# First attention, three entries: where the layernorm's root and its normalised tiles are computed

## The reference

```python
def _layernorm(x, axis=-1, eps=1e-05):
    m = jnp.mean(x, axis=axis, keepdims=True)
    v = jnp.var(x, axis=axis, keepdims=True)
    return (x - m) / jnp.sqrt(v + eps)
...
x = _layernorm(x + _L0_attn_ref(x, ...), axis=-1)
x = _layernorm(x + _L0_ffn_ref(x, ...), axis=-1)
x = _layernorm(x + _L1_attn_ref(x, ...), axis=-1)
x = _layernorm(x + _L1_ffn_ref(x, ...), axis=-1)
```

## Time and profile before

| | us |
|---|---|
| three runs | 1034.5, 1035.62, 1036.26 |
| median | 1035.62 |
| profiled execution, span from first to last instruction | 1033.4 |
| the median less that span | 2.2 |
| first attention in the profiled execution, about | 29 to 299 |

### The profile page before, as it was taken

One profiled execution on the slowest core, in us unless ns is written; L12 is line 12 of the kernel. 1 busy time (PEld: TensorE's weight loads), 2 busy tenths in 40 slices (PEclk: granted clock), 3 DMA queues, 4 the chain that ended last, 5 costly groups with the idle time before them and its releaser, 6 DMA issues.

```text
span 1033.4 us, 18254 instructions
## 1 busy us (share of the span) xinstructions
PE 991.0 (96%) x6658; PEld 826.1 (80%) x6658; DVE 735.9 (71%) x2003; ACT 606.6 (59%) x1177; POOL 371.4 (36%) x646
## 2 busy tenths in 40 slices
PE   8999999989999898889999999999999999999997
PEld 6555655556658897778989999999999999999997
DVE  6676787767638779866557777766776876677764
ACT  5576657664359774455556666455666655466660
POOL 4455474562131574353722223322222232222600
PEclk9899999998999999999999999999999999999999
DMA  7100010012110001022201010010101011010101
GB/s 249 28 2 22 4 35 8 23 60 85 45 65 4 1 8 36 28 76 62 82 1 42 1 41 4 39 42 1 42 1 42 1 42 42 1 42 1 42 24 59
DMA packets 29234, 36.91 MB, mean 36 GB/s; under 512 B 1780, under 2 KB 26584, under 8 KB 29144
## 3 DMA queue, kind: packets, MB, share of 16 engines
q1 hardware_dynamic: 24728, 31.15, 9.5%
q10 hardware_dynamic: 4416, 4.59, 1.4%
HBM read 31.40 MB, written 4.20 MB: 34 GB/s over the span
## 4 chain that ended last, share of the span: by engine, by line
PE 56%; DVE 4%; POOL 2%; issue 1%; ACT 1%; DVEq 0%; POOLq 0%; ACTq 0%
PE ps L1947 25%; PE ps L1964 24%; PE ps L1837 2%; PE ps L1919 2%; DVE ln_stats L2366 1%; PE ps L1977 1%; PE ps L1888 1%; POOL hs L1734 1%; POOL x_b L1734 0%; PE ps L1851 0%; DVE amp L2402 0%; PE ps L1866 0%; PE ps L1879 0%; PE ps L1788 0%; DVE att L2458 0%
## 5 line engine op out<-in xcount | busy, mean ns | idle before, releaser
L2202 ACT ACTIVATE G<-ps,bias_col 128x512 f32<-128x512 f32 x192 | 135.9, 708 | 176.6 <-PE ps L1947 167.9
L1964 PE MATMUL ps<-w_h,G_h 128*128 128x256 f32 x736 | 204.3, 278 | 0.0
L1964 PE MATMUL ps<-w_l,G_h 128*128 128x256 f32 x736 | 204.0, 277 | 0.0
L1964 PE MATMUL ps<-w_h,G_l 128*128 128x256 f32 x736 | 204.0, 277 | 0.0
L2506 DVE TENSOR_TENSOR G_l<-G,G_h 128x512 fp32r<-128x512 f32 x192 | 155.8, 820 | 59.6 <-ACT G_h L2203 59.6
L1764 POOL TENSOR_TENSOR x_a<-xn,mlp_g 128x1024 f32<-128x1024 f32 x20 | 68.0, 3399 | 333.8 <-DVE xn L2534 333.8
L708 ACT ACTIVATE probs<-ps 128x512 f32<-128x512 f32 (+3 forms) x256 | 98.3, 441 | 96.5 <-PE ps L847 95.7
L1947 PE MATMUL ps<-xT_h,w_h 128*128 128x512 f32 x384 | 151.7, 395 | 0.2 <-issue 0.2
L1947 PE MATMUL ps<-xT_h,w_l 128*128 128x512 f32 x384 | 149.9, 390 | 0.0
L1947 PE MATMUL ps<-xT_l,w_h 128*128 128x512 f32 x384 | 149.5, 389 | 0.0
L1124 DVE CUSTOM_DVE_ANT_0 ps<-ps,q_mask 128x128 f32<-128x128 f32 (+3 forms) x256 | 120.8, 512 | 29.5 <-PE ps L836 29.0
(11 more groups left out here) (330 smaller groups left out, 2099.8 us busy)
## 6 DMA issues: line engine op xcount, KB each, us to landing
w_raw<-L_ffn_W_T SPq DMA_DIRECT2D x12, 1024.0 KB, 5.1
hs<-L_attn_hidden_states SPq DMA_DIRECT2D x8, 512.0 KB, 3.9
x_kept<-hs SPq DMA_DIRECT2D x4, 512.0 KB, 4.1
w_raw<-x_kept SPq DMA_DIRECT2D x2, 1024.0 KB, 5.3
out<-xn SPq DMA_DIRECT2D x3, 512.0 KB, 2.8
w_raw<-L_ffn_ent_w_T SPq DMA_DIRECT2D x1, 1024.0 KB, 9.8
w_raw<-L_ffn_ent_pw SPq DMA_DIRECT2D x1, 1024.0 KB, 12.0
heads_T<-neg_rows SPq DMA_DIRECT2D x64, 2.0 KB
```

The lines of the kernel that those rows point to most:

```text
L1964: mm = pe.matmul(ps[:, 4 + t // 2, (t % 2) * D:(t % 2 + 1) * D], x[b % 2][f][:, t * P:(t + 1) * P], w2_chunk(w, f), start=(k == 0), stop=( ...
L2202: act.activation(G32[n % 4], bank, ACT.Gelu, bias=bias)
```

## The change

In entries 1 to 3 of the first attention the layernorm of the batch before is spread over three engines:

- VectorE: one `bn_stats` in each of slots (3,1), (3,2), (4,0), (4,1) and the four `bn_aggr` in (4,2). Its nine root steps and its four `xn` tiles are gone there.
- ScalarE: in slot (4,3) the root, as Ln of variance plus eps and then Exp of -1/2 times that, 4 columns each. At the start the table set that holds both is preloaded, where an Exp instruction stood before.
- GpSimd: the four `xn` tiles, one in each of slots (5,0) to (5,3), after the slot's other steps. Keep tiles move to (6,1), (6,2), (6,3), (7,0), bias tiles from (5,1), (5,2), (5,3), (6,0) to (6,0), (7,1), (7,2), (7,3).

The layernorm of batch 3 after the entries stays on VectorE.

```diff
-BIAS_TILE_AT = ((5, 1), (5, 2), (5, 3), (6, 0))
-KEEP_TILE_AT = ((6, 2), (6, 3), (7, 0), (7, 1))
+STATS_AT = ((3, 1), (3, 2), (4, 0), (4, 1))
+MEAN_AT = (4, 2)
+ROOT_AT = (4, 3)
+NORM_TILE_AT = ((5, 0), (5, 1), (5, 2), (5, 3))
+KEEP_TILE_AT = ((6, 1), (6, 2), (6, 3), (7, 0))
+BIAS_TILE_AT = ((6, 0), (7, 1), (7, 2), (7, 3))
...
+        pool.memset(g.turns[:, 2:3], EPS).then_inc(s["g_eps"], 1)
...
+        def normalised_tile(b, t):
+
+            if t == 0:
+                pool.wait_ge(s["a_root"], b + 1)
+                pool.wait_ge(s["g_x1"], b + 1)
+            ins = pool.tensor_scalar(xn[:, 0, t, :], g.rsum[:, t, :], g.lnw["mv"][:, t, 0:1],
+                                     g.lnw["y"][:, t:t + 1], ALU.subtract, ALU.mult)
+            if t == RT - 1:
+                ins.then_inc(s["v_norm"], 1)
...
+                    if when != "first" and (p, r) in NORM_TILE_AT:
+                        normalised_tile(i - 1, NORM_TILE_AT.index((p, r)))
                     if when != "first" and (p, r) in KEEP_TILE_AT:
...
+        def root(b):
+
+            if b == 0:
+                act.wait_ge(s["g_eps"], 1)
+            act.wait_ge(s["v_mean"], b + 1)
+            act.activation(g.lnw["var"][:, :], g.lnw["mv"][:, :, 1], ACT.Ln, bias=g.turns[:, 2:3]
+                           ).then_inc(s["a_log"], 1)
+            act.wait_ge(s["a_log"], b + 1)
+            act.activation(g.lnw["y"][:, :], g.lnw["var"][:, :], ACT.Exp, scale=-0.5).then_inc(s["a_root"], 1)
...
-        act.activation(wave_phase[:, 2, 0:1], wave_phase[:, 3, 0:1], ACT.Exp)
+        act.preload_act_table_set("natural_log_exp_and_others")
...
+        def row_statistics(i, when, t):
+
+            if t % 2 == 0:
+                v.wait_ge(s["work_read"], WORK.number(i, when, ("out", t // 2)) + 1)
+            ins = v.bn_stats(g.lnw["stats"][:, t, :], g.rsum[:, t, :])
+            if t == RT - 1:
+                chain.step(ins)
+
+        def row_means():
+            chain.settle()
+            for k in range(RT):
+                ins = v.bn_aggr(g.lnw["mv"][:, k, :], g.lnw["stats"][:, k, :])
+            ins.then_inc(s["v_mean"], 1)
...
-                if (p, r) == (4, 0) and when != "first":
-                    norm = normalise(i, when)
-                next(norm, None)
-                next(norm, None)
-            assert next(norm, None) is None
+                if when != "first" and (p, r) in STATS_AT:
+                    row_statistics(i, when, STATS_AT.index((p, r)))
+                if when != "first" and (p, r) == MEAN_AT:
+                    row_means()
```

More of the change, by code:

```diff
@@ L271, in build @@
         g.last_b = put(nc, "last_b", g.small, 20 * D - 80 - D, [D])
-        g.turns = sb(top, nc, "turns", [P, 2])
+        g.turns = sb(top, nc, "turns", [P, 3])
         attention0(nc, A, g, top)
@@ L397, in attention0 @@
              "p_work work_read p_ex ex_read a_xT a_attT a_nT v_xT g_rope g_chain g_val a_stack stack_low "
-             "p_max v_max v_neg m_row0 m_row1 p_score a_exp g_sel p_out a_out v_chain v_norm g_x1 "
+             "g_eps v_mean a_log a_root p_max v_max v_neg m_row0 m_row1 p_score a_exp g_sel p_out a_out v_chain v_norm g_x1 "
              "phase_in v_turn a_sin v_mod mod_out mod_in small_in wave_rows_in path_in gate_in ent_in l1_in last_in "
@@ L765, in entry @@
                         matrix_high(MATRIX_HIGH_AT[p, r])
+                    if when != "first" and (p, r) == ROOT_AT:
+                        root(i - 1)
         def first_copies(t):
@@ L1258, in prepare, with normalise @@
                 yield
[L1260 to L1265, removed]
+        def row_statistics(i, when, t):
[9 more added lines that the diff above has]
+            ins.then_inc(s["v_mean"], 1)
+        def normalise():
+            v.wait_ge(s["v_tail"], 2 * KC)
             yield from layernorm_steps(v, chain, g.lnw, g.rsum, xn[:, 0, :, :], s["v_norm"],
-                                       (s["g_x1"], i))
+                                       (s["g_x1"], B))
         PREPARE_AT = ((1, 2), (1, 3), (2, 0), (2, 1), (2, 2), (2, 3), (3, 2), (3, 3), (4, 0), (5, 1), (5, 3), (6, 1),
@@ L1274, in entry @@
             slots = [(p, r) for p in range(PAIRS) for r in range(RT)]
-            norm = iter(())
             work_ahead = prepare()
@@ L1395, in _ @@
                             x_res[:, 2 * half:2 * half + 2, :], ALU.add).then_inc(s["v_tail"], 1)
-        for _ in normalise(B, "after"):
+        for _ in normalise():
             pass
```

## The result

The changed kernel takes 1039.68 us (median), the kernel before 1035.06 on the same chip: ratio 1.004, 95% interval 1.0027 to 1.0054, so slower by 4.6 us, or 0.4%. The profiled execution of the changed kernel has a span of 1037.9 us, that of before 1033.4: +4.5.

A forecast was written before the change was run, and what follows sets the result against it. TensorE, busy 96% of the span, was taken as the bound, its gaps setting the stage's length. Terms 1.6 + 1.7 + 0.4 - 0.5 + 1.1 = +4.3 us on the median 1035.62 gave 1039.9, range 1036.8 to 1042.7.

The forecast's parts named there:

- The stall: Slot (5,3), entries 1 and 2: three GpSimd tiles delay `k_stack`; TensorE idles some 3.3 us, losing 1.6 and 1.7 us.
- The tile's duration: GpSimd's `xn` tiles in pair 5: 1.22 us each, from eight such tiles in the trace, against 0.52 on VectorE.
- Statistics in pair 3: Slots (3,1) and (3,2), entries 1 and 2: one `bn_stats` in each frees score banks later, 0.2 us lost per entry.
- The clock: Behind slot (5,3): half clock after the idle time in both entries 1 and 2, one stretch more, +1.1 us (-1.1 to +2.2).
- Entry 3: Pair 5 gains about 1 us, the last select in pair 7 loses some 0.45: -0.5, between -1.0 and +0.3.
- The root on ScalarE: Slot (4,3): Ln 0.31 and Exp 0.20, 0.6 us together ahead of exponential (5,0), taken to cost nothing.
- GpSimd's backlog in pairs 6 and 7: Three more bias tiles make selects up to 0.7 us later, but value passes read them two slots later: taken at nothing.
- No further half-clock stretch: Rival, behind slot (5,3): the stall comes without one more slow stretch, 1038.8 us, or 1037.7; chance 0.19.
- Faster: Rival, `k_stack` of slot (5,3): GpSimd's tile is short there, 0.52 us by the line-rate rule, giving 1033.1 us; chance 0.07.
- point of decision: Slot (5,3): at a GpSimd tile of about 0.65 us `k_stack` lets TensorE go on as early as before.

The follow-up runs named there:

- filled run: Changed kernel plus, in entries 1 and 2, thirteen matmuls nobody reads ahead of TensorE's wait for the stack in slot (5,3): 1037.17 us, ratio 1.0012.
- Experiment 4: Changed kernel with all four `bn_stats` of each entry in slots (4,0) and (4,1), two in each, none in pair 3: 1040.64 us, ratio 1.0055.
- one tile ahead: Changed kernel with one GpSimd `xn` tile in slot (5,0), ahead of the stack, and three behind it in (5,3): 1032.87 us, ratio 0.9971.
- tiles on VectorE one per slot: Changed kernel with the four `xn` tiles done by VectorE instead of GpSimd, still one in each of slots (5,0) to (5,3): 1030.70 us, ratio 0.995.
- tiles in one slot: Changed kernel with the four `xn` tiles done by VectorE, all in slot (5,1): 1032.18 us, ratio 0.9965.
- the run with 0.79: Changed kernel with GpSimd doing columns 0 to 127 of each `xn` tile and VectorE the rest in the same slot: 1036.46 us, ratio 1.0013.
- the run with the tiles behind: Changed kernel with all four GpSimd `xn` tiles in slot (5,3), behind that slot's stack and select: 1029.78 us, ratio 0.9941.
- the run with the bias tiles back: Changed kernel with VectorE doing all four `xn` tiles in slot (5,1), and GpSimd's bias and keep tiles where the kernel before has them: 1034.94 us, ratio 0.9997.
- rearranged: Changed kernel with `xn` tiles behind the stack in (5,3), two `bn_stats` moved to (3,3), entry 3's bias tiles in pairs 5 and 6: 1028.77 us, ratio 0.9937.

## Why the prediction was right, point by point

- **The stall** was right in place and cause and nearly in size. Idle time 3.39 and 3.40 us where I said 3.3 (the terms that I gave for it, 1.7 and 1.5, make 3.2). The chain from GpSimd's first tile to the end of `k_stack` took 5.43 us against 5.63: a tile is 1.18 us from start to next start, not 1.22, and GpSimd came to it 0.15 us earlier, not 0.1. The loss at full clock is pair 5 of the filled run, 10.20 and 10.19 us, against 8.81: 1.39 us in each entry where the sum has 1.6 and 1.7.
- **The tile's duration**, taken from eight tiles of a later stage, held: 1.212 to 1.220 us for all twelve. The Trainium skill's GPSIMD Engine Reference, section 4.1, has one-input work on GpSimd at roughly line-rate; for this tile with its two pointers the trace disagrees (0.40 us on VectorE, and 1.217 on GpSimd), and the whole sign of the result hung on it. The 0.52 that I read for VectorE is a mean over four tiles, one of them drawn out by a neighbour (last section).
- **Statistics in pair 3**: +0.17 and +0.27 us, said 0.2. Experiment 4 shows that this is the price of those two `bn_stats`, and that moving them into pair 4 doesn't save it: it comes back in slot (5,0).
- **The clock** is the term that was mis-sized. I wrote +1.1, one stretch more at a price of 1.09, with +2.2 as the upper bound. The filled run gives 1.43 and 2.60 us for the changed kernel. Before, entry 2's pairs 5 and 6 take 18.07 us against entry 1's 16.68, so 1.39 was paid there already: the change adds 2.6 us, more than my bound. Two steps failed: the price, read from slot (6,0) to its end alone, left out the end of pair 5, which was slow too (9.09 against 8.81); and entry 2, where I counted no change, has a slow stretch twice as long as it had (206.40 to 213.10 in the window above, against 201.60 to 205.00).
- **Entry 3**: pair 5 gained 1.37 us (said 1), and the last select costs 0.35 us at the end (said 0.45): from slot (7,0) to the next stage's first matmul it is 5.89 us where it was 5.54, and TensorE now waits for it:

```profile
303.27 0.64 PE L889 MATMUL ps<-probs,val 128*32 128x256 f32 x8 [0.21 <-POOL probs L597]
```

- **The root on ScalarE** costs nothing. Ln and Exp stand ahead of exponential (5,0), no table load between them, and slot (5,0) is 1.74 us where it was 1.77:

```profile
131.69 0.34 ACT L764 ACTIVATE ln_var<-ln_mv,turns 128x4 f32<-128x4 f32 x1
132.07 0.20 ACT L767 ACTIVATE ln_y<-ln_var 128x4 f32<-128x4 f32 x1
132.18 1.07 ACT L725 ACTIVATE probs<-ps 128x512 f32<-128x512 f32 x2
```

- **GpSimd's backlog in pairs 6 and 7**: nothing, as taken; pair 7 is 7.38 us (7.37 before).
- **What the sum did not have.** Of the total, entry 1 (2.94) is the forecast's 2.9, though by other parts (1.39 of stall, 1.43 of clock, 0.17 of statistics); entry 2 is 1.0 us above its 1.9, the stretch up to entry 1 is 0.9 above its zero, and entry 3 is 1.7 below its -0.5. The last two are mostly half-clock stretches that none of my steps touches: one in pair 3 of entry 0 came (7.95 us, 6.41 before; the entry's first score matmul came 0.87 us earlier, which takes back part of it), the one in pairs 0 and 1 of entry 3 went (8.20 and 7.37 us, 9.44 and 7.63 before). Entry 0's pair 3, whose work is the same in all kernels of the table, is 6.4 to 6.5 us in nine of the twelve and 7.9 in three (changed, one tile ahead, tiles on VectorE one per slot); entry 3's pair 0 is 9.4 in three (before, one tile ahead, tiles in one slot) and 8.2 in nine. I can't say what sets them off. So the total of 4.3 against 4.5 is in part luck. By the terms it is: stall 2.8 (said 3.3), statistics 0.4 (0.4), entry 3 -1.0 (-0.5), clock 2.6 (1.1), and some -0.4 that no term had. The mechanism and the sign owe nothing to these errors that cancel.
- **The rivals.** "No further half-clock stretch" is what the filled run built: 1037.17, where I had 1038.8. "Faster" has no row for it: GpSimd's tile is 1.22 us. Its point of decision, 0.65, came from a loss of 1.7; with the 1.39 measured it would be 1.22 less 0.46, 0.76, for pair 5 alone, and the run with 0.79 fits that (8.92 us for pair 5, against 8.81). What a short tile itself would give stays unmeasured; the run with the tiles behind shows what the change is worth with no tile ahead of the stack, 5.7 us, which is more than the 2.5 of that rival.

## What to carry to other kernels

When work moves to an engine that is less busy on the average, look for the step in that engine's own queue which the bounding engine waits for, and count the idle time ahead of that step: here 0.77 us, and what went beyond it was paid in full. The same work one step further back in the queue, behind that step, turned 0.4% slower into 0.6% faster. And price a stall on TensorE with the slow stretch behind it, which here cost nearly as much again (2.6 us) as the stall made the two pairs longer (2.8).

## What the runs showed of the hardware

VectorE and GpSimd drew each other out. In the kernel before, VectorE's tiles begin at 134.47 and GpSimd's bias tile at 134.75; the tile's shortest instruction is 0.399 us and its longest 0.832, and four take 2.08 us, against 1.46 with no bias tile beside them. GpSimd pays too: in the run with the bias tiles back its copy beside the tiles takes 0.43 us and its select 0.48, elsewhere 0.29 and 0.41. The two sets of instructions of VectorE's tile line, before and in one slot without bias tiles (ns, min/median/max):

```profile
L167 DVE TENSOR_SCALAR xn<-rsum,ln_mv,ln_y x16: 399/414/832, 134.5 to 317.5; 128x256 f32<-128x256 f32 x16
```

```profile
L1296 DVE TENSOR_SCALAR xn<-rsum,ln_mv,ln_y x12: 395/401/545, 133.8 to 279.8; 128x256 f32<-128x256 f32 x12
```

The Trainium skill's SBUF — State Buffer, section "Who interferes with whom", says that the two engines share a pair of ports, and that where VectorE's instruction uses that pair beside its own, as a `tensor_scalar` can, whichever engine issued first holds the shared pair for its whole instruction while the other waits. By that rule the long tile waits for the bias tile, and the rows agree: it is 0.43 us longer than the shortest. These are the long tile and the bias tile beside it in the kernel before, then in the run with the bias tiles back; the bias tile begins first, and the long tile ends 0.15 us after it in both:

```profile
134.75 0.78 POOL L619 TENSOR_TENSOR hs<-hs,b_out 128x256 f32<-128x256 f32 x1
134.85 0.83 DVE L167 TENSOR_SCALAR xn<-rsum,ln_mv,ln_y 128x256 f32<-128x256 f32 x1
```

```profile
135.16 0.76 POOL L624 TENSOR_TENSOR hs<-hs,b_out 128x256 f32<-128x256 f32 x1
135.25 0.81 DVE L1296 TENSOR_SCALAR xn<-rsum,ln_mv,ln_y 128x256 f32<-128x256 f32 x1
```

Which ports the tile used, no run here shows.

The other is the clock behind a gap: behind 0.59 to 0.62 us idle at this place (tiles behind the stack, rearranged) slot (6,0) stayed at full clock in four entries of four, behind 0.98 us in two of two, behind 2.05, 2.18 and 3.4 us in none, and behind gaps of 0.93 and 0.94 us in the kernel before it fell in one entry and not in the other. In the run with the bias tiles back gaps of only 0.53 and 0.21 us stand in slot (5,3) of entry 1; there it stayed, and in entry 2 of the same run it fell (pair 6 is 9.40 us). So the length of the gap alone doesn't decide it.
